# First stage of a four-layer convolution kernel: convolution of image n+2 and forward transforms of image n in one step, chunk by chunk

## The reference, cut to what matters

```python
# layer 0: sign of the normalised x, weights in {-1, 0, 1}, 3x3
x = x + conv(sign(_gn(x)), round(tanh(weight))) * alpha
# layer 1, first half: forward transform of the normalised result
x_ft = rfft2(_gn(x), norm='ortho')[:, :, :mlat, :mlon]
```

## Time and profile before

| | us |
|---|---|
| median of three runs | 11926.42 (11920.08 to 11942.38) |
| the profiled execution | 11907.83 |
| its span | 11906.1 |
| first stage in it, to the first work of the next | 1801.26 |

### The profile page before, as it was taken

One profiled execution on the slowest core, in us unless ns is written; L12 is line 12 of the kernel. 1 busy time (PEld: TensorE's weight loads), 2 busy tenths in 40 slices (PEclk: granted clock), 3 DMA queues, 4 the chain that ended last, 5 costly groups with the idle time before them and its releaser, 6 DMA issues.

```text
span 11906.1 us, 291565 instructions
## 1 busy us (share of the span) xinstructions
PE 10400.3 (87%) x120871; PEld 9145.9 (77%) x120871; DVE 7857.5 (66%) x13708; ACT 5940.8 (50%) x7016; POOL 3902.2 (33%) x3240
## 2 busy tenths in 40 slices
PE   6888887884899999999899999999999899999996
PEld 4666667884888888888788888888888788888885
DVE  6667651124577777776777777777776777777775
ACT  4555551110455555555555555555555555555553
POOL 0000000000344444444444444444444444444442
PEclk8999998886999999999999999999999999999997
DMA  7888879994211111111211111111111211111100
GB/s 184 216 217 210 216 187 229 242 245 108 53 36 39 39 37 37 39 39 38 48 38 36 37 36 39 39 39 36 39 39 39 49 36 36 37 37 38 39 22 16
DMA packets 996826, 947.12 MB, mean 80 GB/s; under 512 B 591777, under 2 KB 936849, under 8 KB 979921
## 3 DMA queue, kind: packets, MB, share of 16 engines
q1 hardware_dynamic: 972048, 708.59, 27.5%
q0 software_dynamic: 23488, 220.21, 5.1%
HBM read 605.77 MB, written 322.96 MB: 78 GB/s over the span
## 4 chain that ended last, share of the span: by engine, by line
PE 37%; DVE 17%; ACT 8%; issue 7%; POOL 5%; DMA 1%; SPq 0%; DVEq 0%; POOLq 0%; ACTq 0%
PE c_ps L938 23%; PE c_ps L1009 3%; POOL c_cube L1649 3%; PE c_ps L1087 3%; PE c_ps L1022 2%; PE c_ps L1074 2%; DVE c_v L1451 2%; ACT c_xp L1195 2%; DVE c_xp L1415 2%; DVE c_bn L1395 2%; DVE c_s L1514 2%; DVE c_xr L1433 2%; ACT c_xp L1135 1%; ACT c_sq L1258 1%; DVE c_qt L1489 1%
## 5 line engine op out<-in xcount | busy, mean ns | idle before, releaser
L938 PE MATMUL c_ps<-c_xp,c_wst 128*128 128x224 f16 x45696 | 4908.0, 265 | 154.8 <-DVE c_xp L1415 154.8
L938 PEld LDWEIGHTS c_ps<-c_xp,c_wst 128*128 128x128 f16 x45696 | 4365.1, 98 | 631.6 <-issue 415.5
L1624 POOL TENSOR_TENSOR c_xr<-c_sm,c_xr 128x448 f32<-128x448 f32 x448 | 704.1, 1572 | 2233.2 <-DVE c_xr L1433 2233.2
L1649 POOL TENSOR_TENSOR c_cube<-c_sq,c_qk 128x896 f32<-128x896 f32 x448 | 928.2, 2093 | 1193.2 <-ACT c_sq L1249 1193.1
L1226 ACT ACTIVATE c_qt<-c_ps 128x896 f32<-128x896 f32 x224 | 206.1, 920 | 2050.3 <-PE c_ps L1030 2050.3
L1184 ACT ACTIVATE c_tn<-c_xr,c_nrm 64x448 f32<-64x448 f32 (+1 forms) x832 | 955.2, 1152 | 56.9 <-DVE c_xp L1415 26.9
L1009 PE MATMUL c_ps<-c_wqkv,c_xn 64*128 64x192 f32 x6272 | 793.9, 368 | 200.5 <-DVE c_v L1451 193.0
L528 PE MATMUL b_ps<-b_xs,b_wt 64*64 64x64 f32 x6384 | 805.3, 298 | 179.2 <-DVE b_xj L504 174.6
L1195 ACT ACTIVATE c_xp<-c_tn 128x1080 f16<-128x1080 f32 (+1 forms) x544 | 572.1, 1063 | 731.9 <-DVE c_tn L1408 728.1
L528 PEld LDWEIGHTS b_ps<-b_xs,b_wt 64*64 64x64 f32 x6384 | 762.1, 217 | 182.4 <-issue 182.3
L1415 DVE TENSOR_TENSOR c_xp<-c_tn,c_xp 128x1080 f16<-128x1080 f32 (+1 forms) x544 | 664.2, 1231 | 271.7 <-ACT c_xp L1195 270.7
(11 more groups left out here) (158 smaller groups left out, 17691.7 us busy)
## 6 DMA issues: line engine op xcount, KB each, us to landing
b_wt<-in_L_conv_weight SPq DMA_DIRECT2D x56, 2048.0 KB, 21.8
a_xc<-in_x SPq DMA_DIRECT2D x64, 1568.0 KB, 18.9
x<-a_x1s POOLq DMA_DIRECT2D x32, 3136.0 KB, 22.6
a_xh<-x SPq DMA_DIRECT2D x64, 1568.0 KB
c_xr<-x SPq DMA_DIRECT2D x224, 448.0 KB, 4.0
out<-c_xr SPq DMA_DIRECT2D x448, 224.0 KB, 3.1
xf<-a_freq POOLq DMA_DIRECT2D x32, 1792.0 KB, 17.5
b_xs<-xf SPq DMA_DIRECT2D x28, 2048.0 KB, 24.9
```

The lines of the kernel that those rows point to most:

```text
L938: ins = pe.matmul(sums(c, p), wst[:, ws, pr, FIRST_TAP[p] + k].rearrange("p q o -> p (q o)"), xp[:, xs, PLANE[kind] + f, row:row + CROWS, ...
L1624: pool.tensor_tensor(here, apart(sm[:, half]).unsqueeze(1).to_broadcast([P, 2, CROWS, QW]), here, ALU.add).then_inc(s.added, 1)
L1649: pool.tensor_tensor(cube[:, :, k].rearrange("p q r c -> p r q c"), sq[:, :, :, k], qk[:, :, :, k], ALU.mult).then_inc(done, 1)
```

## The change

`overlapped` is replaced by `staged`. Its step for image n holds the convolution of image n+2, the statistics and signs of image n+3, and the transforms of image n, and runs over the 14 chunks of the convolution:

- PE: in each chunk the six products of the convolution, then one or two of the 23 transform groups (`group_at`). The small product for the mean of image n+3 comes at chunk 10.
- DVE: in each chunk the two evictions of the chunk, the `bn_stats` of the result of the chunk before, and at chunks 4 to 8 three `bn_stats` each of x of image n+3. The steps of the deviation come at chunks 1, 3 and 12.
- ACT: in each chunk the copies of its groups; the four sign passes of image n+3 at chunks 10 to 13.
- SP: the two halves of x of an image are loaded when the upper and the lower half of the chunks are taken out. The turned load goes to one of two `xh` buffers.
- POOL: the result is stored in two halves, at the middle and the end of the convolution, the frequencies in two parts of four and three groups.

In the convolution the first six chunks wait for two of the four sign passes only. The convolution now runs two images ahead of the transforms, so there are two steps without transforms at the start, and two without a convolution at the end. Room for the second `xh` comes from `wpos`, which now lies in `x1s`. Arithmetic, products and bytes are as before.

```diff
-def overlapped(eng, images, prep, conv, rest):
-            prep(2 * t + (2 + odd), odd)
-            conv(2 * t + (1 + odd), 1 - odd)
-            rest(2 * t + odd, odd)
+def staged(eng, images, prep, step):
+    def full(t):
+        for odd in range(2):
+            step(2 * t + odd, odd, True, True, True)
+    prep(0, 0)
+    step(-2, 0, True, True, False)
+    step(-1, 1, True, True, False)
...
+    step(images - 4, 0, True, True, True)
+    step(images - 3, 1, True, False, True)
+    step(images - 2, 0, False, False, True)
+    step(images - 1, 1, False, False, True)
+X_PARTS = (4, 5, 6, 7, 8)
+MEAN_AT = 10
+SIGNS_AT = (10, 11, 12, 13)
+VARIANCE_AT = 1
+CENTER_AT = 12
+FREQ_PARTS = ((0, 4), (4, 7))
...
-        xh = sb("xh", [P, C, W])
+        xh = sb("xh", [P, 2, C, W])
+        group_at = lambda c: range(GROUPS * c // CHUNKS, GROUPS * (c + 1) // CHUNKS)
... SP
+                    for half in range(2):
+                        sp.wait_ge(x1_done, (2 * t + odd) * CHUNKS + CHUNKS // 2 * (half + 1))
+                        load(2 * t + (2 + odd), odd, half)
+                    turn(2 * t + odd, odd)
... POOL
+                if conv:
+                    store_x1(n + 2, 0)
+                if rest:
+                    store_freq(n, 0)
+                if conv:
+                    store_x1(n + 2, 1)
+                if rest:
+                    store_freq(n, 1)
... DVE
+            def x_part(n, odd, lo, hi):
+                if lo == 0:
+                    dve.wait_ge(x_in[odd], 16 * (n + (2 - odd)))
+            def step(n, odd, conv, prep, rest):
+                for c in range(CHUNKS):
+                    if conv:
+                        conv_part(n + 2, odd, c)
+                        if c:
+                            x1_part(n + 2, c - 1)
...
+                    if prep and c in X_PARTS:
+                        i = X_PARTS.index(c)
+                        x_part(n + 3, 1 - odd, 3 * i, min(3 * i + 3, CHUNKS))
... PE
+            def conv_part(n, odd, c):
+                pe.wait_ge(signed, 4 * n + (2 if ROWS * (c + 1) < J // 2 else 4))
+            def step(n, odd, conv, prep_next, rest):
+                for c in range(CHUNKS):
+                    if conv:
+                        conv_part(n + 2, odd, c)
+                    if rest and c == 0:
+                        spread(n, odd)
+                    if rest:
+                        for g in group_at(c):
+                            dft(n, odd, g)
+                    if prep_next and c == MEAN_AT:
+                        prep(n + 3, 1 - odd)
```

More of the change, by code:

```diff
@@ L249, in _, with moments @@
                                     ps[0:C, ky, 0:3 * C].rearrange("c (k o) -> c k o", k=3)).then_inc(w_put, 1)
-            def moments(st, at, before):
+            def moments(bn, st, at, before):
                 dve.wait_ge(at, before + 1)
@@ L259, in moments @@
                                                 ALU.mult, ALU.add)
-            def prep(n, odd):
[L262 to L283, removed]
-                    ins = dve.bn_stats(bn[:, c], x1s[:, ROWS * c:ROWS * c + ROWS].rearrange("p a w -> p (a w)"))
-                ins.then_inc(conv_at, 1)
-                moments(sty[:, odd], conv_at, 2 * n).then_inc(x1_stats, 1)
@@ L288, in rest @@
-            def rest(n, odd):
+            def x_part(n, odd, lo, hi):
+                if lo == 0:
+                    dve.wait_ge(x_in[odd], 16 * (n + (2 - odd)))
+                for c in range(lo, hi):
+                    ins = dve.bn_stats(bnx[:, c], xc[:, odd, ROWS * c:ROWS * c + ROWS].rearrange("p a w -> p (a w)"))
+                if hi == CHUNKS:
+                    ins.then_inc(prep_at, 1)
+            def prep(n, odd):
+                x_part(n, odd, 0, CHUNKS)
+                moments(bnx, stx[:, odd], prep_at, 2 * n).then_inc(x_stats, 1)
@@ new lines, in x1_part @@
+            def x1_part(n, c):
+                dve.wait_ge(x1_done, n * CHUNKS + (c + 1))
+                ins = dve.bn_stats(bn1[:, c], x1s[:, ROWS * c:ROWS * c + ROWS].rearrange("p a w -> p (a w)"))
+                if c == CHUNKS - 1:
+                    ins.then_inc(conv_at, 1)
+            def conv_part(n, odd, c):
+                half, at = divmod(ROWS * c, J // 2)
+                if c % (CHUNKS // 2) == 0 and above_zero(16 * n):
+                    dve.wait_ge(x1_out[half], 16 * n)
+                here = slice(C * half, C * half + C)
+                dve.wait_ge(conv_done, n * CHUNKS + (c + 1))
+                for hp in range(2):
+                    rows = slice(C * hp, C * hp + C)
+                    ins = dve.scalar_tensor_tensor(
+                        x1s[rows, ROWS * c:ROWS * c + ROWS], ps[rows, c % 3, 0:N4].rearrange("p (a w) -> p a w", a=ROWS),
+                        alph[rows], xc[here, odd, 2 * at + hp:2 * (at + ROWS):2], ALU.mult, ALU.add)
+                ins.then_inc(x1_done, 1)
@@ L301, in rest, with deviation @@
                 dve.tensor_scalar(gst[:, 3:4], gst[:, 2:3], -1.0, GN_EPS, ALU.mult, ALU.add).then_inc(x1_var, 1)
+            def deviation(n):
                 dve.wait_ge(x1_std, n + 1)
```

216 lines of the change are left out of this document (125 added, 91 removed).

## The result

| | before | after |
|---|---|---|
| median of four runs each | 11923.25 (11912.4 to 11942.38) | 11765.5 (11758.85 to 11769.75) |
| ratio of the two | | 0.9868 (0.9856 to 0.9879) |
| the profiled execution, its span | 11907.83, 11906.1 | 11769.75, 11767.7 |
| first stage, to the first work of the second part | 1801.26 | 1598.06 |
| second part | 1150.8 | 1177.6 |

The account below looks back on a forecast made before the run. The prediction took a ring of store, turned load and eviction to bound the first stage. 113.5 + 67.5 + 30 x 47 gave 1591, 210 us less: 11907.8 became 11697.5, plus 18.6 makes 11716; range 11610 to 11850.

Parts of the forecast that it names:

- the likeliest case: First stage: the DMA limit holds, 45.5 to 50 us per step, 11671 to 11806 in total; chance 0.58.
- The change touches nothing behind it, so I forecast this stage and take the rest as it is: Opening step: only the first stage is forecast; the parts after it are taken as unchanged.
- 113.5 + 30 x 47 + 67.5: First stage: start until the first full step, 30 full steps of 47 us, then the end; 1591 against 1801.3 before.
- The 47: Steady step (T) of the first stage: transfers in series, 20 + 20 + 7 us, within 45.5 to 51.3.
- the half transfers: First stage: x and result together took 20 us, so half of each was forecast to take 10.
- The ring: First stage before: store 22 us, turned load 29, and the eviction ending beside it, in series, set the 52.9 us period.
- above 0.93 and 235 to 245: Sign expected after the change: DMA share above 0.93 and 235 to 245 GB/s, with steps of about 47 us.
- PE is the limit: Rival for the first stage: PE bounds the step at 42.4 to 45.4 us, most likely 43.5, total 11611; chance 0.17.
- The 28 switches between bf16 and float32 products: PE's alternation of product types per image, costed at nothing; at 0.1 us each PE would be at 45.2.
- the slow case: Rival: DVE stops at chunk 4 for x; a turned load of 38 us makes T 56, total 11986; chance 0.06.
- The third rival: SP's queue keeps its latencies, store landing before the turned load; T 50.7 to 54, 11836 at 51; chance 0.15.
- The added 18.6: Total: the median stood 18.6 us above the profiled execution, so this was added to 11697.5, giving 11716.

## Why the prediction was right, and which step of it failed

The direction, the range and the likeliest case held: 11765.5 lies in 11610 to 11850 and in the likeliest case's own 11671 to 11806, 49.5 us above the 11716 given. The difference is made up of four terms: 7.1 from the stage, 64.8 from the parts behind it, 0.4 around the span and in rounding, and 22.9 less between the profiled execution and the median.

*The step that failed* is the first paragraph's "The change touches nothing behind it, so I forecast this stage and take the rest as it is". It was right by the source and wrong by 64.8 us of time. It is the largest error of the sum. With PE's code behind the first stage at before's remainder, the kernel takes 11711.7, 4 us from the forecast.

*The stage, term by term.* It was to be 113.5 + 30 x 47 + 67.5 = 1591 (the terms given for the 113.5 add up to 39.9 + 2 x 36.4 = 112.7). By the stores of second halves it is 117.7 to the first full step (image 1's store at 117.71), 1415.5 / 30 = 47.2 per step up to image 31's at 1533.23, and 64.8 from there to 1598.06: 4.2 more, 5.5 more, 2.7 less. The mean over all 30 is under the 47.4 of the steady 28, since the last one, which loads no x, took 41.4. The 47 itself was a sum of stretches measured apart, 11.3 MB in 47 us or 240 GB/s; the mixture ran at 241. That the sum held for the whole, though no single transfer kept its own time (see the half transfers), was partly luck: the forecast gave 45.5 to 51.3 as possible and had no row of such a mixture at a full share.

*What bounds it.* The ring was the limit before, and the DMA engines are now: share 1.00 at 241 GB/s, inside the forecast's "above 0.93 and 235 to 245"; the clock was 0.98 and not the 1.0 named. Half the x load brings PE's limit (42.1, forecast 42.4), half the products change nothing. The rival "PE is the limit" is false by both.

*The costs put at nothing.* The 28 switches between bf16 and float32 products cost nothing that shows: in the step above the conv burst ends at 972.1, the next float32 products begin at 971.97, and where PE then stops, the row names the turned image. With half the x, PE's whole step of the same 28 switches takes 42.1 us, under the 42.4 counted without them. DVE's wait for x was allowed up to 2 us and is 2.4; the rule "more than 2 us in each step" for the slow case was set too sharp, since the step stayed at 47.4. What is late next are the two that were named, x at chunk 4 and the turned image at chunk 0.

*The half transfers.* The forecast took half of 20 us for a half store. The steady part shows 10.6 for the one and 23.8 for the other half in the step shown, as long as the whole store took (22 us): in these rows the time of a store follows what is beside it more than its size. The slow case supposed just this store of 20 and more, and its own calculation that this alone costs nothing was right: PE waits 1.8 us per step for the turned image, and less work for PE does not shorten the step, as it would if store and turned load took a fixed time each and closed a ring with it. x is where it hurts, 2.7 us a step if it comes in one piece. The Trainium skill's 2 us for each such DMA (page "DMA: Bandwidth & Descriptors", section "Anatomy of one DMA — SWDGE (gpsimd) path") would have made 11844, an estimate from that figure, if they lay on the path. No run here shows them there: with four stores per image in after the steady part has a DMA share of 1.00 all the same.

*The third rival*, latencies in SP's queue at T 50.7 to 54, did not come about as it stood. The queue waits 23.9 us per step for the store, but other transfers fill the engines meanwhile, as the argument against it had it. The kernel with x in ACT's queue shows it from the other side: without SP's order the store lands sooner, the turned load later, and the stage is 93 us longer (1698.65 against 1605.83).

*The added 18.6* between the profiled execution and the median did not recur: after's profiled execution is the slowest of its four, 4.3 above their median, and that is the 22.9. It hid a third of the missed term; on the profiled executions alone the forecast was 11697.5 and the measurement 11769.75.

## What to carry to other kernels

Before reordering work around transfers, read the DMA share beside the longest engine's busy time: if both are under the period, as 45.5 and 45.7 were under 52.9 here, look for a ring that closes through one buffer, and try first to split the transfer that closes it (111 us here by itself, while the new order alone cost 316). Once the share was 1.00, another queue only moved the wait from one transfer to another, and fewer bytes shortened the step. And time the unchanged parts apart from the changed one: where a stage is written out into an engine's program, its length shifts the code of all that follows, here worth up to 97 us of 10100, which 6 to 134 empty instructions put in or take out.

## What was not expected of the hardware

The position of identical code in PE's program changes its time: 10072.1 to 10169.6 us for the same second and third part, 1.0%, with six instructions making 33.6 of it (10169.6 to 10136.0).

A full set of DMA engines delivered 241 GB/s in after and in the kernel with half the products, and 235 with half the x, while one stretch of before with only x and the result in flight had 320. What the engines deliver when full depends on the mixture, which here has the turned load's 448-byte runs in it (159 GB/s alone), and 0.86 of share at 213 GB/s had nearly told it in advance (213 / 0.86 = 248).

x moved to a queue of its own landed in 14.8 instead of 21.5 us, and the turned load in another queue took 33 to 50 us to its first use instead of 26 to 29 where PE waited for it; the stage became 93 us longer.
